# A fused decoder layer on one core: TensorE's foreign pieces move from behind the weighting to directly behind the exponential's products

## What is computed

```
x += proj( rms( softmax(q1 k1) v - lam * softmax(q2 k2) v ) )     # 16 heads, head width 8: self attention
x += gelu( softmax((LN(x) Wq + bq)(ctx Wk + bk) / 8) (ctx Wv + bv) Wf + bf ) + ctx
x += shared_swiglu(LN(x)) + sum over top 2 of 16 experts of gate * expert_swiglu(LN(x))
```

## Time and profile before

| what | value |
|---|---|
| median of three runs | 610.67 us |
| the profiled execution's own time | 611.33 us |
| its span | 610.1 us |
| mean granted TensorE clock | 0.952 of full |
| TensorE matmul busy | 552.2 us, 91% |
| VectorE, ScalarE, GpSimd busy | 312.4, 258.4, 230.0 us |
| the attention loop | 47.6 to 243.5 us of the span |

### The profile page before, as it was taken

The page is one execution under the profiler, slowest core; times in us unless marked ns, Lnnn a source line. Parts: engine busy times, 40 slices in busy tenths (PEclk is TensorE's granted clock), DMA queues, the critical chain, the costliest instruction groups (busy, mean ns, idle before and its releaser), DMA issues.

```text
span 610.1 us, 10860 instructions
## 1 busy us (share of the span) xinstructions
PE 552.2 (91%) x3780; PEld 376.9 (62%) x3780; DVE 312.4 (51%) x683; ACT 258.4 (42%) x414; POOL 230.0 (38%) x473
## 2 busy tenths in 40 slices
PE   7987979799879887799999989997999999998998
PEld 5543436345536444556676457456999999997447
DVE  5679685597786994664442653110222222222282
ACT  6324454464654644624431300101666666663110
POOL 2436565455744554422001004664244344334000
PEclk8999889799999978789999989999999999999899
DMA  7744365332322238940009906222232333331721
GB/s 247 213 145 125 107 209 158 106 106 83 97 75 71 46 135 82 272 126 0 1 15 352 322 1 189 87 79 95 64 95 87 98 95 89 96 94 62 286 90 49
DMA packets 62197, 72.46 MB, mean 119 GB/s; under 512 B 14816, under 2 KB 55264, under 8 KB 60608
## 3 DMA queue, kind: packets, MB, share of 16 engines
q1 hardware_dynamic: 58160, 60.59, 34.6%
q0 software_dynamic: 3792, 10.39, 4.9%
q10 hardware_dynamic: 192, 0.79, 0.6%
HBM read 45.32 MB, written 26.03 MB: 117 GB/s over the span
## 4 chain that ended last, share of the span: by engine, by line
PE 42%; issue 18%; DMA 12%; DVE 11%; POOL 10%; ACT 4%; SPq 1%; ACTq 1%; POOLq 0%; DVEq 0%
PE ps L603 13%; DMA x_slots<-XN,slot_i 7%; POOL y_rows L1604 7%; PE ps L614 5%; PE ps L432 3%; PE ps L368 3%; DMA pack_k<-qk_parts 3%; PE ps L531 3%; DVE nmax L862 3%; PE ps L512 2%; PE ps L399 2%; PE ps L420 2%; PE ps L497 2%; PE ps L381 1%; POOL goes_to L1598 1%
## 5 line engine op out<-in xcount | busy, mean ns | idle before, releaser
L862 DVE TENSOR_REDUCE nmax<-ps 128x8 f32<-128x1024 f32 x64 | 77.7, 1215 | 37.7 <-PE ps L399 37.3
L659 PE MATMUL ps<-xt,Wn 128*128 128x128 f32 x752 | 93.4, 278 | 0.0
L659 PEld LDWEIGHTS ps<-xt,Wn 128*128 128x128 f32 x752 | 89.3, 195 | 0.3 <-ACT xt L1426 0.2
L1328 ACT ACTIVATE prob<-ps 128x1024 f32<-128x1024 f32 x64 | 65.5, 1023 | 38.0 <-PE ps L420 38.0
L1604 POOL DMA_INDIRECT y_rows<-yo,goes_to x47 | 45.9, 976 | 83.9 <-DVE yo L1117 83.6
L1109 DVE TENSOR_TENSOR ht<-sa,ps 128x256 f32<-128x256 f32 x47 | 19.8, 420 | 105.6 <-PE ps L670 95.5
L603 PE MATMUL ps<-xT,W1s 128*128 128x512 f32 x128 | 64.4, 628 | 3.4 <-DVE yo L1117 1.9
L1419 ACT ACTIVATE sil<-ps 128x512 f32<-128x512 f32 x32 | 19.1, 597 | 109.7 <-PE ps L603 109.7
L1439 ACT ACTIVATE Wn<-W 128x1024 f32 x47 | 49.7, 1057 | 29.7 <-issue 29.7
L603 PE MATMUL ps<-xT,W2s 128*128 128x512 f32 x128 | 61.0, 599 | 0.0
L614 PE MATMUL ps<-W3s,hTs 128*128 128x256 f32 x256 | 56.5, 381 | 3.5 <-DVE hTs L1040 3.5
(11 more groups left out here) (184 smaller groups left out, 856.8 us busy)
## 6 DMA issues: line engine op xcount, KB each, us to landing
W<-in_L_ffn_routed_w_dram SPq DMA_DIRECT2D x12, 1024.0 KB, 11.7
pack_q<-qk_parts SPq DMA_DIRECT2D x48, 128.0 KB, 3.0
xg<-x_slots SPq DMA_DIRECT2D x47, 129.0 KB, 2.1
x_slots<-zero SPq DMA_DIRECT2D x11, 512.0 KB, 10.6
qk_parts<-part SPq DMA_DIRECT2D x21, 256.0 KB, 2.8
pack_k<-qk_parts SPq DMA_DIRECT2D x42, 128.0 KB, 3.1
yg<-y_rows SPq DMA_DIRECT2D x4, 1024.0 KB, 8.8
X<-in_x_dram SPq DMA_DIRECT2D x4, 512.0 KB, 7.0
```

Of the source, the lines that this page charges most:

```text
L659: r = t.matmul(ps[:, 2 + p, h * P:(h + 1) * P], Wn[:, n % 3, k, h * P:(h + 1) * P], xt[:, p, k, :], start=(k == 0), stop=(k == KT - 1))
L862: v.tensor_reduce(nmax[:, s % 4, a, :, :], ps[:, b:b + 2, :].rearrange("p m (h t) -> p m h t", h=4), AX_X, ALU.max, negate=True).then_inc( ...
L1328: a.activation(prob[:, n:n + 2, :], ps[:, 2:4, :], ACT.Exp, scale=HD ** -0.5).then_inc(exped, 1)
```

## The change

Inside the loop of TensorE's program the call of `between` moves: from the end of each half step to the place behind `exps`. Nothing is added or removed, and no other engine's program is touched.

```diff
             for s in range(STEPS):
                 exps(s, 0)
+                between(s, 0)
                 if s + LEAD < STEPS:
                     scores(s + LEAD, 0)
                 if s:
                     pv(s - 1, 1)
-                between(s, 0)
                 exps(s, 1)
+                between(s, 1)
                 if s + LEAD < STEPS:
                     scores(s + LEAD, 1)
                 pv(s, 0)
                 if s + LEAD - 1 < STEPS:
                     turn_max(s + LEAD - 1)
-                between(s, 1)
             pv(STEPS - 1, 1)
```

## The result

The changed kernel takes 634.1 us (median of 4 runs, 631.2 to 636.6) against 609.95 of the kernel before beside it: a ratio of 1.039 with an interval of 1.033 to 1.045, slower. The forecast was 624 with a range of 609 to 634: the sign is right, and the median lies 0.1 us above the range's upper end. The loss is 24.1 us, not 13. The profiled execution took 636.6 us, the longest of the four; its span is 635.4, its granted clock 0.946.

What follows compares the result with a forecast made beforehand. Only TensorE's order in the 195.9 us attention loop changes, with 28.2 us of waiting to win or enlarge. Profiled 611.3 + 10.9 of walked lateness + 2 of clock = 624.2, so 624 us; range 609 to 634.

Steps and rivals of the forecast that it cites:

- Effect (1): Half steps with a piece: it covers waits for VectorE's maxima, 0.85 us in 19 and 1.29 in 33; both could go.
- Effect (2): Half steps without a piece behind one with: their wait changes, net gain some 0.2 us each, 0.5 over 6 to 10.
- Effect (3): VectorE gets scores a piece later, ahead of its heavy items: +1.8 us at half steps 10 to 13, likewise in 20 to 24.
- Effect (4): Pieces with only just ready inputs, at eleven places, lose the cover of `scores` and `pv`, 0.9 us.
- The end: Half steps 57 to the loop's end, where few scores are left: -1.6 us.
- the waits, walked as +10.9: Walk of all 64 half steps of the loop: how much later `exps` come, together +10.9 us.
- the clock, +2: TensorE's granted clock in the loop: more waits above 1.6 us than before cost +2 us, with 0 and +10 as ends.
- the shifts did not cancel (1): Rival: pieces and `scores` all shift alike, so waits are only paid elsewhere; 611 us, within 5; chance 0.17.
- the cover did not win (3): Rival: pieces cover waiting `scores`, winning 7.3 us and part of ScalarE's lateness; 604 us; chance 0.10.
- Rival 2: Waits in the loop grow as forecast and the clock drops six more times at 2 us: 634, at least 630; chance 0.11.
- the wait of 1.40: Wait at 208.9 in the earlier trace that left the clock at 1.00; cited against more clock drops.
- TensorE stands while VectorE reads its banks: Reading of the waits of `scores` for VectorE's maxima, among them 0.85 us in half step 19 and 1.29 in 33.

Runs made afterwards that it cites:

- ten put back (1): Changed kernel with the pieces (`between`) of half steps 3, 16, 26, 29, 36, 38, 39, 40, 48, 59 back behind the weighting: 625.5 us, 1.027.
- with filler (6): Changed kernel with transposes of the identity, read by nobody, put into the waits of twelve half steps: 622.8 us, 1.023.
- ten alone moved (2): Kernel before with only the pieces of half steps 3, 16, 26, 29, 36, 38, 39, 40, 48, 59 moved behind `exps`: 623.2 us, 1.023.
- weighting first (10): Kernel before with every half step reordered to `exps`, `pv`, piece, `scores`: 687.6 us, 1.126.
- cover alone (11): Kernel before with the piece moved behind `exps` only in half steps 19 and 33: 606.2 us, 0.992.
- experiment 9: Kernel before with the piece moved behind `exps` only in half steps 10 and 26: a single profiled execution of 613.95 us, read for its rows.
- experiment 3: Changed kernel with `scores` put ahead of the piece, giving `exps`, `scores`, piece, `pv`: 630.8 us, 1.036.
- experiment 4: Changed kernel with `turn_max` moved directly behind `exps` of odd half steps, ahead of the piece: 625.1 us, 1.024.
- experiment 7: Kernel before with filler transposes in the waits of half steps 12, 18, 42 and 55: 607.85 us, 0.998.
- experiment 8: Kernel before with `turn_max` moved directly behind `exps` of odd half steps, ahead of `scores` and weighting: 616.7 us, 1.016.
- experiment 5: Changed kernel with eighteen half steps' pieces put back behind the weighting, 27 staying moved: 620.2 us, 1.021.

## Why the prediction was right, and what its sum missed

Lateness of `exps` against the kernel before, gathered by stretch of half steps, in us, from the profiled executions:

| half steps | forecast | changed kernel | ten put back (1) | with filler (6) |
|---|---|---|---|---|
| 0 to 6 | +1.7 | +5.7 | +1.6 | +3.5 |
| 6 to 10 | -0.5 | +0.3 | +0.3 | +0.3 |
| 10 to 13 | +1.8 | +2.0 | +2.0 | +1.4 |
| 13 to 18 | +1.2 | +1.1 | +0.6 | -0.6 |
| 18 to 21 | -1.0 | -2.2 | +0.3 | -1.6 |
| 21 to 24 | +1.3 | +1.1 | +1.1 | +1.1 |
| 24 to 27 | +2.1 | +4.2 | +1.7 | +2.6 |
| 27 to 34 | +0.6 | +1.5 | +0.4 | +1.5 |
| 34 to 37 | +2.1 | +4.1 | +1.7 | +2.6 |
| 37 to 39 | +0.9 | +1.1 | +0.8 | +1.1 |
| 39 to 48 | +0.5 | +2.4 | -0.4 | +1.0 |
| 48 to 57 | +1.8 | +3.3 | +2.8 | +1.7 |
| 57 to the end | -1.6 | +0.7 | +0.1 | -1.1 |
| sum | +10.9 | +25.1 | +13.1 | +13.5 |

The loop in the profiled executions, in us (busy and waiting are TensorE's; the last column has how much of the loop is at the lower clock, and TensorE's busy time in it):

| kernel | loop | busy | waiting | at the lower clock |
|---|---|---|---|---|
| before | 195.9 | 167.7 | 28.2 | 34.2 (31.6) |
| changed | 221.1 | 177.5 | 43.6 | 44.4 (37.0) |
| ten put back (1) | 209.0 | 174.3 | 34.7 | 37.5 (30.8) |
| ten alone moved (2) | 211.5 | 173.8 | 37.7 | 44.4 (40.8) |
| changed, with filler (6) | 209.5 | 181.9, filler with it | 27.6 | 6.8 (6.0) |
| weighting first (10) | 277.6 | 209.6 | 68.1 | 126.3 (114.0) |
| cover alone (11) | 191.6 | 165.2 | 26.4 | 23.9 (22.1) |

Effect (1), cover: right. The waits of 19 and 33 are gone, and experiment 11 shows that this much of the change is a gain by itself, with the clock behind the wait as the larger part of it.

Effect (2), half steps without a piece behind one with: wrong in sign and small, -0.5 forecast, +0.3 measured. The waits came as walked, 0.80 in half steps 7 and 9 where 0.85 was said, but the next `exps` come 2.34 and not 2.28 behind: the seam behind `turn_max`, which a wait used to hide, takes that gain, and the even seams of 6 and 8 come on top.

Effect (3), VectorE a piece late: right in place and size at half steps 10 to 13 (+2.0 for +1.8; +2.0 again in experiment 9). Its reason was half of the truth. I had given the lateness to `scores`; by experiment 3 the weighting, through `turn_o`, holds the same queue and is enough alone (+1.7 in these half steps, with the scores early).

Effect (4), the pieces that wait: right, but the list is too short. In front of the ten TensorE waits 15.7 us in all where it waited 4.2. The price of 0.9 holds for one place alone (experiment 9); in the changed kernel it goes from 0.1 more in half step 39 to 1.6 in 26, 1.9 in 29 and 2.3 in 3. The text counts eleven places and names ten, and the trace has five more that it does not name: 4, 20, 24, 34 and 56, with 0.80, 1.02, 1.01, 0.62 and 1.22 in front of the piece and nothing before. The first four wait for ScalarE's copies behind `copy_max`, by experiment 4; the prediction had walked this queue for half step 36 alone.

The end, -1.6 forecast and +0.7 measured, is a miss: half step 59 waits 2.0 for VectorE, and that took what the missing scores gave.

**The steps that failed by size.** The loss in the loop is 25.2 us where the sum has 12.9. First, the durations of the moved groups were taken as theirs wherever they stand. The walk put 0.24 and 0.07 between groups, and in the new order these are 0.33 and 0.16: the seams, some 7.1 us, were in no term and in no bound. They are most of the 9.8 by which the busy time grew. Second, the waits, walked as +10.9, measured as +15.4, which is 4.5 short: the waits for ScalarE that (4) does not name, and half steps 0 to 6, where the transposes of half step 3 start after a wait of 3.22 us and not of 0.90. Third, the clock, +2, came as 2.7 by the estimate above and was nearly right. Together 15.4 + 7.1 + 2.7 = 25.2. The division is by one profiled execution of each kernel; in half step 0 of the changed one, for instance, a projection takes 3.51 and not 1.96 us at the lower clock, behind a wait of 1.25 that both kernels have.

That the prediction is right by its number is in part luck. Its range reached 634 for a reason that did not come true, six more drops of the clock, and what filled it was mostly the seams and the unnamed waits. Its sign and its places are not luck: experiments 1, 2 and 9 bear them out.

Of the rivals, the shifts did not cancel (1), and the cover did not win (3): it needed less than 0.4 us of new wait at each of the ten places, and they have 1.15 on average. Rival 2 gave 634, which is the time that came, but not by its mechanism: there is one more stretch at the lower clock, not six, and the seams have the larger part of what the forecast lacked. That waits cost a second time is true, as experiments 6 and 10 show (11 us back with filler in them; 41.9 us of longer busy time beside 39.9 of waiting), but the kernel before pays most of that too. The argument against it, the wait of 1.40 in the earlier trace rows, rests on a row that ends with the wait; the trace has the clock at 1.00 behind it as well, until 219.42.

Two more readings of the rows. TensorE stands while VectorE reads its banks: with a piece in other banks put into such a wait the two half steps of experiment 11 won 4 us, of which the covered waits are 1.8 and the clock the rest; in the whole loop it did not win, since here many of the pieces put in between had to wait too. And the clock fell after one wait and not after another; the changed kernel shows the same. The wait of 0.80 in front of half step 16's piece is followed by a piece of 1.99, at a clock of 1.00. Of the longer ones some were followed by a lower clock and some were not: the wait of 1.61 in half step 26 is followed by a piece of 3.50, but the one of 1.94 in half step 29 by a piece of 1.99, and the one of 2.53 in half step 18 by no slow stretch before 145.13, 26 us later. The length of the wait alone does not decide.

## What to carry to other kernels

Where engines work in order and feed one another in a ring, as here, give the others their work first, all the groups that they wait for, and your own independent work last; move such work ahead only in the single places where your next group would wait and the moved one would not. For each piece that moves, ask what it reads and which engine's queue makes that, and list every one. Before moving groups on TensorE, count how often the tiling of the array changes in each order and price each change, as read here at about 0.1 us. And price a wait twice, once for itself and once for the clock that may fall behind it; if it can't be removed, filler in it may give the second part back (11 us in experiment 6, nothing that the runs can tell in experiment 7). When you take such a saving as a share of a change's loss, first ask how much of it the kernel before would have given as well.

## What the runs showed of the hardware

- What follows `exps` at full clock mostly starts 0.23 us behind it if it is on the same 64-row tiles and 0.33 if it is on other tiles; what follows `turn_max` starts 0.07 behind it if it is on the whole array as well and 0.16 if it is on 64-row tiles. A half step with two such changes more took 3.31 us instead of 3.07, in the changed kernel and in experiment 8. No run isolates the tiling from the order.
- Filler transposes in twelve waits raised the mean granted clock from 0.946 to 0.975 and took 11 us off the changed kernel; in four waits of the kernel before they took off no more than the runs can tell (607.85 against 610.3).
- In the changed kernel a wait of 2.53 us (half step 18) and one of 1.94 (half step 29) left the granted clock at 1.00, one of 1.61 (half step 26) was followed by 3.4 us at 0.50.
- A small transfer was issued 1.9 us after its data was there, behind eight others on SyncE's queue, and turned up as a wait of 2.07 us once TensorE was early enough to meet it (experiment 5).
